# Selective scan: rows of B by transfers, dt times u copied into PSUM per half, next projections two steps sooner

## The reference

```
xz = x @ in_proj_w ; u, z = split(xz)
u  = silu(causal_conv4(u) + conv_b)
dt, B, C = split(u @ x_proj_w)           # ranks 16, 16, 16
dt = softplus(dt @ dt_proj_w + dt_proj_b)
for each token:                           # a scan over time
    s = s * exp(dt * A) + (dt * u) * B    # s: 512 channels x 16 states
    y = sum over the 16 states of s * C
y = (y + u * D_skip) * silu(z)
out = y @ out_proj_w ; then rmsnorm and a three-layer MLP
```

## Time and profile before

| | us |
|---|---|
| median of three runs | 3063.63 (3054.53 to 3069.89) |
| the profiled execution | 3064.54 |
| its span, first to last instruction | 3062.8 |
| loads, conv and dt of the first group | 0 to 74 |
| the scan (256 steps) | 74 to 1290 |
| busy over the span: PE, DVE, ACT, POOL | 2634.2, 1982.3, 1502.1, 1328.2 |

### The profile page before, as it was taken

One profiled execution on the slowest core, in us unless ns is written; L12 is line 12 of the kernel. 1 busy time (PEld: TensorE's weight loads), 2 busy tenths in 40 slices (PEclk: granted clock), 3 DMA queues, 4 the chain that ended last, 5 costly groups with the idle time before them and its releaser, 6 DMA issues. The chain is left out here.

```text
span 3062.8 us, 44136 instructions
## 1 busy us (share of the span) xinstructions
PE 2634.2 (86%) x14825; PEld 1554.6 (51%) x14825; DVE 1982.3 (65%) x4366; ACT 1502.1 (49%) x3296; POOL 1328.2 (43%) x1269
## 2 busy tenths in 40 slices
PE   3778988888898989889999968888979998997588
PEld 1224343434343534357777745556645655565355
DVE  1999888888878787816766656777634444454234
ACT  4665666666665656333333324444445555555121
POOL 1676666666666666514333223444451221211200
PEclk8989999999999999989999978999679998997688
DMA  3221111111111111101000143333030000000000
GB/s 119 62 59 57 55 55 56 55 56 52 56 52 53 52 56 52 49 26 40 1 1 1 21 79 68 64 57 66 13 92 10 19 15 15 19 17 25 28 4 4
DMA packets 97042, 128.56 MB, mean 42 GB/s; under 512 B 19841, under 2 KB 54786, under 8 KB 96818
## 3 DMA queue, kind: packets, MB, share of 16 engines
q1 hardware_dynamic: 94834, 122.86, 15.2%
q0 software_dynamic: 960, 2.62, 0.3%
q10 hardware_dynamic: 1024, 0.26, 0.1%
HBM read 86.84 MB, written 13.37 MB: 33 GB/s over the span
## 5 line engine op out<-in xcount | busy, mean ns | idle before, releaser
L368 POOL TENSOR_TENSOR ma_seen<-ma_state,ma_cs 128x1024 f32<-128x1024 f32 x256 | 602.7, 2356 | 416.3 <-DVE ma_state L972 416.2
L972 DVE TENSOR_TENSOR_SCAN ma_state<-ma_decay,ma_last,ma_drive 128x512 f32<-128x512 f32 x512 | 651.9, 1273 | 0.0
L585 PE MATMUL ma_acc<-ma_seen,ident 128*128 128x512 f32 x1024 | 497.9, 612 | 58.9 <-POOL ma_seen L368 58.9
L958 DVE TENSOR_TENSOR ma_drive<-ma_wdt,ma_spread 128x512 f32<-128x512 f32 x512 | 354.9, 693 | 204.5 <-PE ma_spread L571 143.0
L833 ACT ACTIVATE ma_decay<-ma_dt,ma_a_neg 128x512 f32<-128x512 f32 x512 | 337.7, 707 | 41.8 <-POOL ma_dt L415 41.7
L585 PEld LDWEIGHTS ma_acc<-ma_seen,ident 128*128 128x128 f32 x1024 | 195.6, 195 | 281.5 <-issue 180.0
L2068 DVE CUSTOM_DVE_ANT_0 sw_score<-sw_score,both_band 128x256 f32<-128x256 f32 (+1 forms) x512 | 197.5, 447 | 95.1 <-PE sw_score L1890 78.9
L822 ACT ACTIVATE ma_last<-ma_state,ma_goes_on 128x2 f32<-128x2 f32 x255 | 74.4, 292 | 305.2 <-DVE ma_state L972 304.5
L2013 ACT ACTIVATE sw_prob<-sw_turned 128x512 f32<-128x512 f32 (+1 forms) x256 | 135.5, 581 | 172.2 <-PE sw_turned L1904 132.8
L104 POOL TENSOR_TENSOR moe_h_low<-both_V,light_wqkv 128x512 fp32r<-128x512 f32 x80 | 104.9, 1311 | 247.5 <-DVE light_wqkv L100 240.0
L1812 POOL TENSOR_SCALAR_AFFINE_SELECT sw_prob<-sw_prob 128x512 f32<-128x512 f32 x128 | 84.3, 658 | 247.3 <-ACT sw_prob L2013 247.3
(11 more groups left out here) (483 smaller groups left out, 5760.3 us busy)
## 6 DMA issues: line engine op xcount, KB each, us to landing
ma_cs<-c_rows SPq DMA_DIRECT2D x256, 256.0 KB, 3.2
both_wide<-both_kh SPq DMA_DIRECT2D x28, 192.0 KB, 4.0
both_wide<-both_qh SPq DMA_DIRECT2D x20, 256.0 KB, 4.9
x_rows<-X SPq DMA_DIRECT2D x1, 4096.0 KB, 14.7
light_rows<-li_y SPq DMA_DIRECT2D x32, 128.0 KB, 1.7
out_dram<-li_o SPq DMA_DIRECT2D x32, 128.0 KB, 1.8
X<-in_L_attn_x_dram SPq DMA_DIRECT2D x1, 3584.0 KB, 13.0
both_QP<-both_qh SPq DMA_DIRECT2D x12, 256.0 KB, 4.8
```

Of the source, the lines that this page charges most:

```text
L368: g.tensor_tensor(out=seen[n % RR][:, :, :], in0=state[n % SR][:, :, :], in1=each(cs[n % CR][:, :], 2), op=ALU.mult).then_inc(S["seen_full ...
L585: ins = t.matmul(accs(mm), K["ident"][:, :], seen[n % RR][:, mm, :], start=False, stop=(n % NS == NS - 1))
L958: v.tensor_tensor(out=drive[mm][:, :], in0=wdt[:, m, :], in1=spread[n % 2][:, :], op=ALU.mult)\
L972: v.tensor_tensor_scan(state[n % SR][:, mm, :], decay[s % DR][:, :], drive[mm][:, :], last[:, k, m:m + 1], ALU.mult, ALU.add).then_inc(S[" ...
```

## The change

- Rows of B come by transfers as those of C do: `stores` writes both (bc_rows), `b_spread(n)` reads a row to 128 partitions into a ring `bs` of three; the ring of C falls from four to three (CR = 3). On SP the order is c(n), [the store at q 28], b(n+2).
- PE's `spreads`, the three bf16 parts and the work for them on ACT and POOL go. The two PSUM banks of `spread` become `weight`.
- wdt holds one half instead of two. ACT copies it into the two banks `weight` (`moves`): for the second half at q 15, for the next group's first half at q 31. A drive reads weight (PSUM) and bs (SBUF).
- On POOL dt_log, dt_sum and dt_weight of the next group's first half stand at q 27, 28, 29.
- The gates units on PE stand at q 6 to 9 (before 7 to 10), turn1 at 10 (12), project at 12 to 15 (13, 14, 16, 17), the taps one step sooner; ACT empties the gates at 7 to 10, takes turn1 at 11, the projections at 13 to 16, and does the Silu of the gates at 17 (12). turn1 comes before turn2 in the order of the banks.

```diff
-DR, SR, RR, CR = 6, 4, 4, 4
+DR, SR, RR, CR = 6, 4, 4, 3
...
+        order += first[:DH]
         if one:
             order += [("turn2", i - 1, k) for k in range(DH)]
-        order += first
+        order += first[DH:]
...
-        dt, wdt = A.sb("dt", [P, MB, GN]), A.sb("wdt", [P, MB, GN])
-        bcp = [A.sb(f"bcp{k}", [96, GN], BF16) for k in range(2)]
+        dt, wdt = A.sb("dt", [P, MB, GN]), A.sb("wdt", [P, 2, GN])
...
-        spread = [A.ps(f"spread{k}") for k in range(2)]
-        drive = [A.ps(f"drive{k}") for k in range(2)]
+        weight, drive = ([A.ps(f"{n}{k}") for k in range(2)] for n in ("weight", "drive"))
...
-                sp.dma_start(c_rows[f], dbc[NS:2 * NS, :]).then_inc(S["c_stored"], 16)
-                sp.wait_ge(S["c_stored"], 16 * (f + 1))
+                sp.dma_start(bc_rows[f], dbc[0:2 * NS, :]).then_inc(S["rows_stored"], 16)
+                sp.wait_ge(S["rows_stored"], 16 * (f + 1))
+
+            def b_spread(n):
+                i, q = divmod(n, Q)
+                since(sp, "drive_done", 2 * (n - CR + 1))
+                sp.dma_start(bs[n % CR][:, :], bc_rows[i, q % NS:q % NS + 1, :].to_broadcast([P, GN])).then_inc(b_in[n % CR], 16)
+
+            def c_spread(n):
+                i, q = divmod(n, Q)
+                since(sp, "seen_full", n - CR + 1)
+                sp.dma_start(cs[n % CR][:, :], bc_rows[i, NS + q % NS:NS + q % NS + 1, :].to_broadcast([P, GN])).then_inc(c_in[n % CR], 16)
 
             stores(0)
...
+            b_spread(0)
+            b_spread(1)
+            for n in range(Q * GROUPS):
+                c_spread(n)
+                if n % Q == Q - 4 and n // Q < LAST:
+                    stores(n // Q + 1)
+                if n + 2 < Q * GROUPS:
+                    b_spread(n + 2)
...
             def dt_weight(i, h):
                 pool.wait_ge(S["dt_done"], 2 * i + h + 1)
-                since(pool, "drive_done", 2 * (Q * (i - 1) + NS * (h + 1)))
-                g.tensor_tensor(out=half(wdt, h), in0=half(dt, h), in1=half(u, h), op=ALU.mult).then_inc(S["wdt_done"], 1)
+                since(pool, "w_moved", 2 * (2 * i + h))
+                g.tensor_tensor(out=flat(wdt[:, :, :]), in0=half(dt, h), in1=half(u, h), op=ALU.mult).then_inc(S["wdt_done"], 1)
...
                     if front and q == 26:
                         dt_rest(i + 1, 0)
+                    if front and q == 27:
+                        dt_log(i + 1, 0)
                     if front and q == 28:
-                        dt_log(i + 1, 0)
+                        dt_sum(i + 1, 0)
                     if front and q == 29:
-                        dt_sum(i + 1, 0)
-                    if front and q == 30:
                         dt_weight(i + 1, 0)
...
-                    if n + 1 < Q * GROUPS:
-                        spreads(n + 1)
...
-                    if q in (7, 8, 9, 10):
-                        gates(i, q - 7)
+                    if q in (6, 7, 8, 9):
+                        gates(i, q - 6)
+                    if q == 10 and front:
+                        turn1(i + 1, 0)
+                        turn1(i + 1, 1)
...
-                    if q in (13, 14, 16, 17) and front:
-                        project(i + 1, (13, 14, 16, 17).index(q))
+                    if q in (12, 13, 14, 15) and front:
+                        project(i + 1, q - 12)
...
+            def moves(i, h):
+
+                n = Q * i + NS * h
+                act.wait_ge(S["wdt_done"], 2 * i + h + 1)
+                for mm in range(2):
+                    since(act, "drive_done", 2 * n - 1 + mm)
+                    a.activation(weight[mm][:, :], wdt[:, mm, :], ACT.Copy).then_inc(S["w_moved"], 1)
+
...
                     if n:
                         keeps(n - 1)
+                    if q == NS - 1:
+                        moves(i, 1)
+                    if q == Q - 1 and front:
+                        moves(i + 1, 0)
                     if n + 2 < Q * GROUPS:
                         decays(n + 2)
...
                 if mm == 0:
-                    dve.wait_ge(S["b_spread"], n + 1)
-                    if q % NS == 0:
-                        dve.wait_ge(S["wdt_done"], 2 * i + h + 1)
+                    dve.wait_ge(b_in[n % CR], 16 * (n // CR + 1))
+                if q % NS == 0:
+                    dve.wait_ge(S["w_moved"], 2 * (2 * i + h) + mm + 1)
                 since(dve, "scan_done", s - 1)
-                v.tensor_tensor(out=drive[mm][:, :], in0=wdt[:, m, :], in1=spread[n % 2][:, :], op=ALU.mult)\
-                 .then_inc(S["drive_done"], 1)
+                v.tensor_tensor(out=drive[mm][:, :], in0=weight[mm][:, :], in1=bs[n % CR][:, :], op=ALU.mult).then_inc(S["drive_done"], 1)
...
-                            for m, first in enumerate((30, 32, 36, 38)):
+                            for m, first in enumerate((28, 30, 33, 35)):
```

More of the change, by code:

```diff
@@ L267, in mamba_phase @@
         seen = [A.sb(f"seen{k}", [P, 2, GN]) for k in range(RR)]
-        cs = [A.sb(f"cs{k}", [P, GN]) for k in range(CR)]
+        bs, cs = ([A.sb(f"{n}{k}", [P, GN]) for k in range(CR)] for n in ("bs", "cs"))
         last = A.sb("last", [P, NS, MB])
@@ L274, in mamba_phase @@
         dbc = xs1[0:48, 0:2, :].rearrange("p j d -> p (j d)")
[L275 to L276 removed]
         pre = lambda h: (ramp, ex)[h]
[L278 removed]
+        bc_rows = nc.dram_tensor("bc_rows", (GROUPS, 2 * NS, GN), F32).ap()
         acc = A.ps("acc", (P, 2 * GN))
         accs = lambda mm: acc[:, mm * GN:(mm + 1) * GN]
[L281 to L282 removed]
+        weight, drive = ([A.ps(f"{n}{k}") for k in range(2)] for n in ("weight", "drive"))
         bank = [A.ps(f"bank{k}") for k in range(2)]
@@ L347, in _ @@
             for k in range(CR):
-                sp.wait_ge(c_in[k], 16 * Q * GROUPS // CR)
+                for came in (b_in, c_in):
+                    sp.wait_ge(came[k], 16 * len(range(k, Q * GROUPS, CR)))
         @block.gpsimd
@@ L392, in finishes @@
                 g.tensor_tensor(out=shift3[:, :], in0=shift3[:, :], in1=rstd3[:, :], op=ALU.mult).then_inc(S["shift3_done"], 1)
[L394 to L401, removed]
             def dt_rest(i, h):
@@ L562, in outputs @@
                 fill(ins, "out", i, k)
[L564 to L572, removed]
             def starts(i, h):
@@ L723, in rows_out @@
                 a.activation(dbc, out[0:48, :], ACT.Copy).then_inc(S["dbc_out"], 1)
-            def b_high(f):
-                act.wait_ge(S["dbc_out"], f + 1)
-                a.activation(bcp[f % 2][0:32, :], dbc[0:32, :], ACT.Copy).then_inc(S["b_high"], 1)
-            def b_mid(f):
-                act.wait_ge(S["b_rest"], f + 1)
-                a.activation(bcp[f % 2][32:64, :], rest, ACT.Copy).then_inc(S["b_middle"], 1)
-                a.activation(part[:, :], rest, ACT.Copy).then_inc(S["b_mid"], 1)
-            def b_low(f):
-                act.wait_ge(S["b_rest2"], f + 1)
-                a.activation(bcp[f % 2][64:96, :], rest, ACT.Copy).then_inc(S["b_low"], 1)
             def steps_raw(f, m):
@@ L864, in body @@
                         scaled2(i - 1)
-                    if q in (8, 9, 10, 11):
-                        gates_out(i, q - 8)
-                    if q == 12:
-                        if one:
-                            turned2(i - 1, 0)
-                            turned2(i - 1, 1)
-                        if front:
-                            turned1(i + 1, 0)
-                            turned1(i + 1, 1)
+                    if q in (7, 8, 9, 10):
+                        gates_out(i, q - 7)
+                    if q == 11 and front:
+                        turned1(i + 1, 0)
+                        turned1(i + 1, 1)
+                    if q == 12 and one:
+                        turned2(i - 1, 0)
+                        turned2(i - 1, 1)
+                    if q == 13 and front:
+                        halos(i + 1)
+                    if q in (13, 14, 15, 16) and front:
+                        projected(i + 1, q - 13)
+                    if q == 17:
                         gates(i)
-                    if q == 13 and two:
+                    if q == 17 and two:
                         normalized(i - 2)
-                    if q == 14 and front:
-                        halos(i + 1)
-                    if q in (14, 15, 17, 18) and front:
-                        projected(i + 1, (14, 15, 17, 18).index(q))
                     if q == 20 and front:
@@ L921, in _ @@
             act.wait_ge(S["a_neg"], 1)
+            moves(0, 0)
             decays(0)
```

34 lines of the change are left out of this document (5 added, 29 removed).

## The result

The changed kernel takes 2936.11 us (median of four runs, 2923.2 to 2955.2) against 3066.76 of the kernel before beside it; ratio 0.959, 95% interval 0.951 to 0.968. One of the four runs of the kernel before took 3780.07 us, in a slow state of the chip: it is in that median and not in the ratio, and the median of the other three is 3063.63. The forecast was 2935, the range 2905 to 3000. The profiled execution took 2947.91 us with a span of 2946.1, so 116.7 us of span less, where the sum said 129. That the median came within 1.1 us of the forecast is luck: single runs of the changed kernel lie 32 us apart, and the sum itself is 12 us off.

The account below looks back on a forecast made before the run. DVE was taken to set the pace, standing 162 us inside the scan. 162 - 15 (boundary) - 17 (ACT behind PE) - 3 (taps) + 2 (start) = 129 us off 3064.5: 2935.5, median 2935; range 2905 to 3000.

Parts of the forecast that it names:

- the sum: Whole kernel: 162 - 15 (boundary) - 17 (ACT behind PE) - 3 (taps) + 2 (start) = 129 us less.
- Spreads off PE: DVE's waits for PE's spread, some 129 us, go; PE's work per group is 122 us against DVE's 132.
- ACT behind PE: Groups 2 to 7: ACT empties PE's banks late, delaying decays; DVE stands 2.8 us at step 10, 17 in all.
- The boundary: At q 31 DVE waits 2.2 us for wdt and ACT's copy, seven times: 15 us, against 25 before.
- B by transfers: 256 more transfers of 256 KB on SP's queue, landing in 3.2 us; nothing on the path.
- the drive's operands: DVE's drive still reads one operand from PSUM, one from SBUF: 0.69 us kept, bounds 0.61 and 0.71.
- the copies of q 15: ACT's copies for the second half have about 1 us to spare before DVE wants the first; costed at nothing.
- Sooner projections, later Silu: DVE's wait for conv input, 7.7 us, leaves 3; Silu at step 17 costs nothing, at worst 1 us a group.
- rival 1: PE's clock drops in its burst, costing 26 to 48 us over six groups: 2961 to 2983; chance 0.17.
- Rival 2: PE sets the pace, as ACT, POOL and PE wait in order and rings don't absorb it: 2995; chance 0.10.
- Transfers late: B's rows come late, landing at 11 us or more: slower, near 3165 at 12 us; chance 0.03.
- waits that only move to the same size: Copies at q 15 and 31 late by as much as the spreads before: within 0.5%; chance 0.02.

Follow-up runs that it names:

- run 4: Changed kernel with one bf16 matmul of zeros (0.22 us) added on PE in each step, DVE never waiting for it; ratio 0.963, scan stretch 1121.4 us.
- runs 7 to 9: Changed kernel with: dt_weight and copies sooner; statistics later; statistics, outputs and gates banks later. Scan stretch 1095.0, 1097.1, 1095.6 us (changed kernel 1097.4).
- run 10: Changed kernel with ACT emptying the last hidden1 bank at q 25, ahead of dt's exponential, not at q 26; ratio 0.954, scan stretch 1074.7 us.
- Run 8: Changed kernel with DVE's four bn_stats at q 11 and 12 instead of 9 and 10; scan stretch 1097.1 us (changed kernel 1097.4).
- runs 5 and 6: Changed kernel with dt_weight at q 28 on POOL; changed kernel with q 31's copies before the third hidden2 bank on ACT. Scan stretch 1097.4 and 1097.2 us.
- run 1: Kernel before with only dt_log, dt_sum and dt_weight one step sooner on POOL; ratio 0.986, scan stretch 1180.8 us (kernel before 1213.6).
- run 2: Changed kernel without the copies into PSUM: wdt holds both halves, drives read both operands from SBUF; 3194.81 us, ratio 1.041 to the kernel before.
- run 3: Changed kernel with gates, turn1, projections, Silu and taps at their old steps; ratio 0.968, scan stretch 1116.3 us.

## Why the prediction was right, point by point

**Spreads off PE.** Right: all of the spread's waits are gone, and the price was place more than work (run 4: 24 us for the work, against 129 us of waits). The sentence that PE "catches up in each group and its queue alone holds nothing" was wrong. 122 us of work against 132 is a balance over the group; from body 26 to the projections PE has no pause, and the end of that run decides how far groups 2 to 7 lie above DVE's own 133.7 us: three edits that removed waits gave 0 to 2 us (runs 7 to 9), one that let the run start sooner gave 22.6 (run 10). No run puts the spreads alone back into the changed kernel, so how much of the 116 us is theirs and how much the other parts' is not measured directly.

**ACT behind PE.** 17 us forecast, 17.1 measured in six waits. The place was q 9 and not 10: the statistics ask for the outputs bank before the decays are missed. I had not looked at the statistics. Run 8 shows the decays as the next to ask. The length of PE's run was counted right within 0.1 us, in the sum of its parts.

**The boundary.** 15 us forecast, 16.0 measured. It counted wdt alone. The ACT queue ended at the same time (runs 5 and 6), so the number was right with half of the reason, and that is luck: ACT's half was not in the sum. The copy took 0.593 us (0.6). That the 25 us of before were wdt's was half true (run 1): under 3.5 us for wdt lay 1.6 us for the spread.

**B by transfers, the drive's operands, the copies of q 15.** Right at nothing: landing 3.2 us, drives 0.697, no wait at q 15 or 16. The Trainium skill (ScalarE: Activation LUTs, the remark on destinations) holds ScalarE's path to PSUM to be the quicker one; no run here shows it: the copy took 0.593 us into PSUM and 0.589 out of it. The contention of run 2 decides this change, and the prediction left it out, since the drive keeps one PSUM operand.

**Sooner projections, later Silu.** Costed at 5 us off for the taps and nothing for the Silu; together the new places are worth 19 (run 3), since with the old ones ACT, behind its Silu, is late at q 15. The wait for the conv input was 5.5 us, not 3.

**The sum.** Of the 12 us between 129 and 116.7: taps 2.5, boundary 1.0, three short waits of 0.5 that were not in the sum 1.4, the part behind the scan 1.7. The largest, 6, is DVE's own time: the stretch less its waits was 1051.4 us before and is 1057.3 after. In steps without a wait the pace is the same (3.90 us a step in both). DVE's gaps that are too short to be listed, all between a scan and the drive behind it, add up to 21.6 us in 351 before and to 26.8 in 392 after. So 41 waits of before had taken in a short gap, some 0.13 us each, and 162 us of listed idle were worth 156. The adding up of two waits that are one debt did no harm here, since I had put DVE's place at q 10 behind the boundary's delay.

**Rivals.** The clock stayed at 1.00 through the run but for its first 3 us (rival 1 fell; run 1 shows it at work before). Rival 2, PE as the pace, gave 2995, 59 us too long, but its mechanism, that the rings don't absorb PE's lateness, is the one that runs 7 to 10 show, between q 26 and q 14. Transfers late, and waits that only move to the same size, did not come.

## What to carry to other kernels

A wait in front of an instruction tells who asked first, not what the time is spent on. Take the wait away and see whether the stretch gets shorter, or find the engine that has no pause for most of a group and let that run start sooner. Where an engine serves another at one step's distance behind long work, move the service to something that isn't in that queue; the price is the place, not the 0.22 us. And when an operand moves to SBUF, look at what the other operand is and at what POOL reads at that time; the damage shows in the lengths of instructions, not in the list of waits.

## What the runs showed of the hardware

- DVE's multiply of 128x512 with both inputs in SBUF took up to 2.85 us (median 1.47) beside POOL's instructions, and POOL's multiplies from SBUF 2.77 instead of 2.36; without one beside it 0.67 to 0.70. With one input in PSUM it took 0.67 to 0.70 throughout. With both in SBUF, one that began during POOL's weigh never ended before it (250 of 250, run 2).
- ACT copies 128x512 f32 from SBUF to PSUM in 0.593 us, as from PSUM to SBUF (0.589).
- Twice the transfers of 256 KB on one queue, at 0.39 of the DMA engines instead of 0.18, land as fast, in 3.2 us.
- PE was at half clock for 13.7 us behind a visible wait of 1.36 us at the start of groups 5 to 7 of the kernel before, for 6.8 us in group 4 and not in groups 2 and 3, and not at all there once that wait was gone (run 1).
